# Picture statistics ahead of the effective weights, first token statistics one stage earlier, a smaller fill of ones

## The reference, cut to what matters

```python
# patch tokens: one mean and variance per picture
mu  = mean(x, axis=(1, 2, 3)); var = var(x, axis=(1, 2, 3))
xn  = (x - mu) * rsqrt(var + 1e-5) * ln_w + ln_b          # (16, 3, 96, 96)
xc  = einsum('bchw,oc->bohw', xn, w) + conv_b             # 1x1 convolution over 3 channels
tokens = patches(xc) @ proj_w.T + proj_b + pos_emb        # (16, 36, 192)
h = concatenate([tokens, txt], axis=1)                    # (16, 548, 192)
# first attention: layer norm of every token, then q, k, v and random features
h = h + performer(layernorm(h))
...                                                       # gated attention, talking heads, experts
```

## Time and profile before

| | |
|---|---|
| median of 3 executions | 4711.84 us (4711.47 to 4717.4) |
| the profiled execution's own time | 4714.95 us |
| its span | 4713.2 us |
| PE busy | 4591.7 us (97%) |
| DVE, ACT, POOL busy | 52%, 47%, 33% |
| patch stage | up to 63.5 us |
| first matmul of the performer's keys | 70.81 us |
| granted PE clock, mean | 0.991 |

### The profile page before, as it was taken

The page is one execution under the profiler, slowest core; times in us unless marked ns, Lnnn a source line. Parts: engine busy times, 40 slices in busy tenths (PEclk is TensorE's granted clock), DMA queues, the critical chain, the costliest instruction groups (busy, mean ns, idle before and its releaser), DMA issues. The chain is left out here.

```text
span 4713.2 us, 139432 instructions
## 1 busy us (share of the span) xinstructions
PE 4591.7 (97%) x57406; PEld 3808.2 (81%) x57406; DVE 2459.3 (52%) x7376; ACT 2201.9 (47%) x5115; POOL 1543.9 (33%) x2393
## 2 busy tenths in 40 slices
PE   6999999999989999999999999999999999999998
PEld 4667776766668888888888888888888888899998
DVE  5665555667555555555555555545555554442333
ACT  3443443555545554554555455455545544212444
POOL 1100003776643333333333333333333332001555
PEclk8999999999999999999999999999999999999999
DMA  4112110000000000000000000000000000232333
GB/s 108 24 30 48 37 30 7 1 2 2 1 13 2 13 13 2 20 13 2 13 13 13 2 13 13 2 13 13 13 2 13 13 2 13 71 95 67 64 65 56
DMA packets 122451, 110.64 MB, mean 23 GB/s; under 512 B 63959, under 2 KB 110380, under 8 KB 121828
## 3 DMA queue, kind: packets, MB, share of 16 engines
q1 hardware_dynamic: 94431, 66.34, 6.1%
q0 software_dynamic: 16768, 23.59, 2.8%
q10 hardware_dynamic: 10628, 11.80, 1.1%
HBM read 59.76 MB, written 41.48 MB: 21 GB/s over the span
## 5 line engine op out<-in xcount | busy, mean ns | idle before, releaser
L2191 PE MATMUL PS<-th_kT,th_qg 64*125 64x274 f32 x10560 | 1417.8, 400 | 0.0
L1897 POOL TENSOR_TENSOR th_qg<-th_qT,w_th_th 128x180 f32<-128x180 f32 x1760 | 848.0, 504 | 1615.3 <-PE PS L2191 1605.5
L2090 ACT ACTIVATE th_P<-PS 110x600 f32<-110x600 f32 x880 | 647.6, 736 | 1116.8 <-PE PS L2178 1116.8
L2008 DVE TENSOR_REDUCE th_nmx<-PS 125x1 f32<-125x548 f32 x880 | 641.4, 729 | 901.8 <-PE PS L2191 901.8
L2178 PEld LDWEIGHTS PS<-th_mixn,th_P 61*110 61x110 f32 x17600 | 981.8, 173 | 96.7 <-issue 20.0
L2191 PEld LDWEIGHTS PS<-th_kT,th_qg 64*125 64x125 f32 x10560 | 942.4, 184 | 139.3 <-issue 0.2
L2178 PE MATMUL PS<-th_mixn,th_P 61*110 61x60 f32 x17600 | 977.1, 254 | 2.8 <-ACT th_P L2090 1.8
L2100 ACT ACTIVATE th_P<-PS,th_nb 125x548 f32<-125x548 f32 x880 | 621.5, 706 | 106.7 <-DVE th_nb L2011 106.7
L1330 POOL TENSOR_SCALAR ga_P<-ga_P,ga_rw 110x110 f32<-110x110 f32 (+4 forms) x240 | 265.6, 1118 | 159.6 <-DVE ga_rw L1498 158.7
L2011 DVE TENSOR_SCALAR th_nb<-th_nmx,w_th_b 125x1 f32<-125x1 f32 x880 | 240.1, 273 | 32.2
L2216 PEld LDWEIGHTS PS<-th_P,th_v 110*32 110x32 f32 x11520 | 230.2, 110 | 29.1 <-issue 28.1
(11 more groups left out here) (356 smaller groups left out, 6269.1 us busy)
## 6 DMA issues: line engine op xcount, KB each, us to landing
pf_xT<-pf_spill SPq DMA_DIRECT2D x32, 412.5 KB, 5.4
ex_tokens<-th_xn SPq DMA_DIRECT2D x124, 82.5 KB
pf_spill<-pf_xT SPq DMA_DIRECT2D x16, 412.5 KB, 3.7
ex_turned<-th_rT SPq DMA_DIRECT2D x16, 412.5 KB, 3.1
ex_x<-ex_turned SPq DMA_DIRECT2D x32, 206.2 KB, 4.0
out_h<-X SPq DMA_DIRECT2D x16, 330.0 KB
ex_w<-in_L_ffn_W ACTq DMA_DIRECT2D x18, 288.0 KB
ex_w<-in_L_ffn_W ACTq DMA_DIRECT2D x8, 576.0 KB
```

Of the source, the lines that this page charges most:

```text
L1897: ins = pool.tensor_tensor(qg[:, m % SB, :, 64 * s:64 * s + HQ].rearrange("p c (h n) -> p c h n", n=QH), qT[:, im % 2, :, at + s * QH:at + ...
L2008: dve.tensor_reduce(nmx[:, p:p + 1], PS[0:MR, bank:bank + 2, 0:HK], AX.XY, ALU.max, negate=True) \
L2090: act.activation(P2[:, :, :, at * QT:(at + 1) * QT].rearrange("p t h (s n) -> p s (t h) n", s=2), PS[0:R, MB:MB + 2, 0:VO].rearrange("p s ...
L2191: ins = pe.matmul(PS[0:MR, bank + a, 0:HK], qg[s, p, c, 0:MR], kT[s, im % 2, c, :], start=c == 0, stop=c == NC - 1)
```

## The change

Four edits:

1. In the patch stage DVE takes the picture statistics first. The nine instructions for `weff` are cut into `weigh(0)`, `weigh(1)` and `weigh(2)`, one for each channel, and these stand where DVE used to wait for PE's average, where it used to wait for POOL's power, and behind the shift.
2. The token statistics of images 0 and 1 (tiles 0 to 9) move from the performer's start to the patch stage's end. DVE takes those of image 0 ahead of `place(4)` and those of image 1 ahead of `place(5)`. Ahead of the first it waits for the text (`text_in`) and for the first three pictures' DMAs (`placed_first`).
3. POOL's power for image 0 moves into the patch stage, between the DMAs of pictures 14 and 15.
4. The fill of `v1` with ones writes only the columns that keep a one, 144 elements per partition in place of 2448.

In the performer DVE begins with `norm(0)` and `norm(1)`, and then takes statistics of tiles 10 and 11.

```diff
+def token_stats(k, dve, tiles):
+    pf = k.pf
+    for u in tiles:
+        dve.bn_stats(pf.st[:, u, :], k.X[:, u, :]).then_inc(pf.stat, 1)
+    for u in tiles:
+        dve.wait_ge(pf.stat, u + 1)
+        dve.bn_aggr(pf.mv[:, u, :], pf.st[:, u, :]).then_inc(pf.aggr, 1)
+    b = tiles[-1] // T
+    dve.wait_ge(pf.aggr, T * (b + 1))
+    dve.tensor_scalar(pf.ve[:, b, :], pf.mv[:, T * b:T * b + T, 1], 1e-5, None, ALU.add).then_inc(pf.var, 1)
...
@@ patch_tokens, gpsimd
-                    pool.dma_start(X[0:NPATCH, b * T, :], y[j * NPATCH:(j + 1) * NPATCH, g, :]).then_inc(placed, 16)
-                pool.wait_ge(placed, 16 * B)
+                    pool.dma_start(X[0:NPATCH, b * T, :], y[j * NPATCH:(j + 1) * NPATCH, g, :]) \
+                        .then_inc(placed if g else placed_first, 16)
+                    if b == B - 2:
+                        pool.wait_ge(pf.var, 1)
+                        pool.tensor_tensor(pf.rstd[:, 0, :], pf.ve[:, 0, :], k.mhalf[0:R, 0:T], ALU.pow).then_inc(pf.powed, 1)
+                pool.wait_ge(placed, 16 * (B - G3))
@@ patch_tokens, vector
-                dve.wait_ge(proj_in, 32)
-                for c in range(CH):
+                def weigh(c):
+                    dve.wait_ge(proj_in, 32)
                     for o in range(CH):
...
                 dve.tensor_tensor(mv[:, :, 1], mv[:, :, 1], sq[:], ALU.add).then_inc(stats, 1)
+                weigh(0)
                 dve.wait_ge(averaged, 1)
...
                 dve.tensor_scalar(var[:], var[:], 1e-5, None, ALU.add).then_inc(varied, 1)
+                weigh(1)
                 dve.wait_ge(powed, 1)
                 done(dve.tensor_tensor(shift[:], avg[:, :, 0], rstd[:], ALU.mult))
                 dve.tensor_scalar(shift[:], shift[:], -1.0, None, ALU.mult).then_inc(shifted, 1)
+                weigh(2)
                 dve.wait_ge(w_in, 16 * (2 + G3))
...
+                dve.wait_ge(text_in, 16 * (T + 1))
+                dve.wait_ge(placed_first, 16 * G3)
+                token_stats(k, dve, range(0, T))
                 place(dve, NG3 - 2)
+                token_stats(k, dve, range(T, 2 * T))
                 place(dve, NG3 - 1)
@@ performer, gpsimd
-                pool.wait_ge(var, 1)
-                pool.tensor_tensor(rstd[:, 0, :], ve[:, 0, :], k.mhalf[0:R, 0:T], ALU.pow).then_inc(powed, 1)
-                pool.wait_ge(powed, 1)
                 pool.memset(e[:, :, :, 2 * M:PW], 1.0).then_inc(filled, 1)
                 pool.wait_ge(filled, 2)
-                pool.memset(v1[:, :, :, W34:VW], 1.0).then_inc(filled, 1)
+                pool.memset(v1[:, :, :, W34:VW].rearrange("p i j (a d) -> p (i j) a d", d=HV)[:, :, :, HD], 1.0).then_inc(filled, 1)
@@ performer, vector
-                for u in range(T):
-                    stats(u)
-                for u in range(T):
-                    aggregate(u)
-                for u in range(T, 12):
-                    stats(u)
-                for u in range(T, 10):
-                    aggregate(u)
                 norm(0)
                 norm(1)
+                for u in range(2 * T, 12):
+                    stats(u)
```

More of the change, by code:

```diff
@@ L175, in early_weights @@
     pf.eps = sb(pf_ctx, "pf_eps", [128, 1])
+    pf.st = sb(pf_ctx, "pf_st", [R, B * T, 6])
+    pf.mv = sb(pf_ctx, "pf_mv", [R, B * T, 2])
+    pf.ve = sb(pf_ctx, "pf_ve", [R, B, T])
+    pf.rstd = sb(pf_ctx, "pf_rstd", [R, B, T])
+    pf.stat, pf.aggr, pf.var, pf.powed = (nc.alloc_semaphore("pf_" + n) for n in ("stat", "aggr", "var", "powed"))
 def late_weights(k, ctx):
@@ L251, in patch_tokens @@
         centred, scaled, normed = sem("centred"), sem("scaled"), sem("normed")
+        placed_first = sem("placed_first")
         turned, xT_in, prod, added, placed = sem("turned"), sem("xT_in"), sem("prod"), sem("added"), sem("placed")
@@ L572, in sb @@
             return ctx.enter_context(nc.sbuf_tensor("pf_" + name, shape, F32))
[L574 to L577, removed]
+        st, mv, ve, rstd = k.pf.st, k.pf.mv, k.pf.ve, k.pf.rstd
         xn = sb("xn", [R, 4, NC, 2, PC])
@@ L604, in sem @@
             return nc.alloc_semaphore("pf_" + name)
-        stat, aggr, var, powed, xn_in = (sem(n) for n in ("stat", "aggr", "var", "powed", "xn_in"))
+        stat, aggr, var, powed = k.pf.stat, k.pf.aggr, k.pf.var, k.pf.powed
+        xn_in = sem("xn_in")
         turned, xT_in = (sem(n) for n in ("turned", "xT_in"))
```

## The result

Twenty runs of each kernel: the changed one has a median of 4704.94 us (4701.55 to 4718.63), the one before 4714.41 us (4711.37 to 4717.4). The ratio is 0.9984, 95% interval 0.9977 to 0.9991, that is 4.2 to 10.8 us less, where 8.85 less (0.9981) was forecast and 4703.0 was named. The ratio is one of means, and three of the twenty executions of the changed kernel took 4716.7 to 4718.6 us, as long as before; the medians lie 9.5 us apart. The kernel is faster, by about the 0.2% that divides "faster" from "no change": the ratio puts it inside "no change", the medians on the edge.

What follows compares the result with a forecast made beforehand. PE, busy for 97% of the span, was taken as the bound, so only an earlier first key product counts: 4.6 - 0.85 + 5.1 = 8.85 us off 4711.84 gives 4703.0 us, with 4699 to 4707.5 for 8 in 10.

Steps and rivals of the forecast that it cites:

- PE's first key product decides, and what it gains arrives: Performer's start: any microsecond by which PE's first key product (70.81 us) comes earlier should arrive at the end.
- Edit 1, 4.6 us: Patch stage, statistics before weights: 2.2 us of covered waits and 2.4 us of earlier start, 4.6 us gained.
- The stage's end, 0.85 us lost: Patch stage's end: moved statistics and POOL's power delay picture 15's DMA from 59.39 to 60.25, a 0.85 us loss.
- The performer's start, 5.1 us: Performer's start: norm(0) begins at once, first key product 2.2 us behind the start in place of 7.3, 5.1 us gained.
- The clock's case: Rival, chance 0.17: shorter PE idle time between stages and an earlier clock rise save 1 to 3.5 us more.
- Engines blocking each other: Rival, chance 0.15: power and weigh(1) block each other (1.36 us), or POOL's fills hold up norms (up to 1.05 us).
- Slower by the clock: Rival, chance 0.04: later stage boundaries meet PE's clock otherwise; 36 us more at 0.50 would give 4721.3 us.

Runs made afterwards that it cites:

- bigfill: The changed kernel with POOL filling all 2448 elements of v1 again; median 4704.2 us, ratio to before 0.9979.
- late: The changed kernel with weigh(1) moved behind the shift, so DVE idles beside POOL's power; median 4706.9 us, ratio to before 0.9978.
- fill: The kernel before with only the v1 fill cut to 144 elements from 2448; median 4710.8 us, ratio to before 0.9994.
- tail: The changed kernel with image 1's statistics behind place(5) and POOL's power behind picture 15's DMA; median 4704.0 us, ratio to before 0.9972.
- tail2: The kernel of tail run once more; median 4700.8 us, ratio to before 0.9975.

## Why the prediction was right

**PE's first key product decides, and what it gains arrives.** Right. From there on the distance between the profiles of before and after stays 11.3 us through the performer's first half, and 10 to 12 until the stretch at 1265 us. In the other profiles the distance to before moves by up to 3 us on the way there, where the clock's stretches differ.

**Edit 1, 4.6 us.** Right in size. Waits covered and steps kept: 14.27 us from first statistics to multiply, where 31.8 - 17.4 = 14.4 was worked out. The pictures' landing changes from execution to execution: the first `bn_stats` starts between 15.92 and 17.82 in ten profiles, with 17.0 or so in the middle, and 17.4 was taken (its 0.9 us for last arrival and wake-up measured 0.8 to 1.3, from the end of the queue's last packet); the weights of before start at 18.81 to 19.75 in three. With the middle values, 19.03 + 16.64 against 17.0 + 14.27, the edit is worth 4.4 us. The changed kernel's own profile drew the earliest landing and before's the latest, and this makes 1.8 of its 11.4 us.

**The stage's end, 0.85 us lost.** Right in mechanism and nearly in size: 0.74 us between the triple and the last DMA, 0.07 more to the start. But the whole loop doesn't show it (22.93 for 23.00), as the clock gave it back. That the two cancel is luck: the sum held the loss and not the gift.

**The performer's start, 5.1 us.** 7.29 - 2.11 = 5.18. That the fill holds up the small addition and not the norms, and that it costs nothing beside key products, bigfill showed.

**The clock's case** (chance 0.17) came half true. PE's work at 32.29 met a rise of the clock at 36.7, 4.4 us behind its start, in before 6.1 us behind (38.49 to 44.6), and bias products took 3.76 us for 4.05, the next transposes 0.72 for 1.29: some 0.8 us. In the performer nothing changed: 7.11 for 7.08 us. Typical values added up, 70.1 - 60.6 (19.03 + 16.64 + 22.98 + 4.13 + 7.29 against 17.0 + 14.27 + 23.0 + 4.21 + 2.11), give 9.5 us, the difference of the medians. The 0.6 us above my sum are the clock's 0.8 us in the patch stage, less some 0.2 at the landings. That the totals agree to the tenth is luck all the same: stretches of the lower clock further on move single profiles by up to 3 us, and the ratio of means gives 7.5.

**Engines blocking each other** (0.15): shown wrong, by late for the power and by bigfill for the fills. The Trainium skill's rule ("SBUF — State Buffer", "Who interferes with whom" and the summary table) of a full block between a two-input DVE instruction and a GpSimd one that reads SBUF does not describe this pair: 0.1 us.

**Slower by the clock** (0.04): the mechanism is real, as the profile after shows, 28 us at 0.51 and some 11 us lost (from 10.1 us ahead of before to 1.2 behind). It stood in three of ten profiles of kernels with the new start and does not shift the median, but it does the mean. Why the clock falls there in some executions stays open; PE was busy for only 23.5 of 28 us there at the full clock, so it is a place with pauses.

## What to carry to other kernels

Put work that nobody awaits yet into the waits of a chain that crosses engines, and price it as the waits covered plus the earlier start; here that was right to 0.2 us. Behind the last DMA of a stage the barrier leaves room: small work belongs there and not ahead of the DMA. Before trusting one profile's total, compare where the clock was low: one stretch of it hid the whole gain. And before crediting an edit with a small gain, look at how soon the clock rose: in fill and tail that was worth more than the edit.

## What was not expected of the hardware

- PE idle for 6.4 us at a stage's boundary cost up to 2.3 us behind it, by key products at the lower clock (7.11 against 4.84); idle transposes of 0.11 us each (40 in 4.53) across the pause saved it. How much it costs changes with when the clock rises: 5.83 to 5.91 us in tail and tail2.
- A fill by POOL held up an addition of 110x5 until it ended, on 110 partitions (1.68 us) as on one (0.42 us, beside the 1x440 fill), and not two norms of 110x384 with a repeated input (1.25 us for two, with and without). The same addition took 0.17 us with no fill beside it.
- The same loads land up to 1.9 us apart from one execution to the next (15.92 to 17.82), as much as a fifth of this change's effect.
